# Local attention step with its scale transposes, reciprocals and maxima in another order

## The chip, the cores and the metric

The kernel runs on one core of one Trainium2 chip. The metric is the device time of one execution in microseconds (us). Four compute engines and the DMA queue (SP) each work through a program of their own, in order, and meet only at semaphores: TensorE (PE in the profile, PEld for its weight loads), VectorE (DVE), ScalarE (ACT) and GpSimd (POOL).

## The reference

The input `x` is 4096 x 256. It is layer-normalised to `xn`. A global causal attention with 16 heads of 16 gives `s`. Two layers of local attention with an MLP, each on `xn` or on the result of the layer before, give `g` through a SiLU. The output is `x + s * g`. Everything is float32. The change lies in the local attention, which in the reference is, for each of the two layers:

```python
h = shift_token(x)                    # second half of the features comes from the token before
q, k, v = split(h @ wqkv)             # 8 heads of 64
q = l2norm(q) * qs                    # divided by the root of the sum of squares over the head
k = l2norm(k) * ksc
q, k = rotary_xpos(q, k)
# windows of 128 queries look at their own and the previous 128 keys, masked
attn = softmax(q @ k.T * 8 + mask)
x = x + (attn @ v) @ wo
```

## The kernel before

The program has these parts one after another: projection of the global attention, global attention, local attention layer 1, MLP 1, local attention layer 2, MLP 2, and the gate at the end. Only `local_attention_layer` (called twice) is touched.

It takes the 4096 tokens in 16 steps of 256 (`NI = 16`, two windows of 128 each) and is a software pipeline: each engine has a written-out loop `for k in range(NI + 4)`, and in step `k` it does the projections of tokens `k`, the scale factors and the scores of tokens `k - 1`, and the attention and the output product of tokens `k - 4` and `k - 3`. The order inside the step is written by hand for each engine. Heads are worked on in two halves, `q = 0` and `q = 1`. PSUM is full: `SU` (four banks) holds scores, `BP[0]` and `BP[1]` hold in turn projected queries and keys, their scale factors and the weighted values, and `B6` and `B7` are used in turn for sums, transposes, V and the output product. Each use of a bank waits on the semaphore of the one before.

What each engine does in step `k`, in the order before the change:

- TensorE: `score_max(2k-3)`, the plain scores from which row maxima are taken (L1048); transposes of X into `B7` (L1181); `weigh(k-4, 1)`, the values weighted by the exponentials and their sums for the second half (L1151, sums in `B6`); `score_turned(2k-5)`, the scores once more, keys by queries, with the maxima subtracted (L1065, L1072); `turn_max(2k-3)`, transposes of the maxima into `B7` (L1086); the scale transposes of step `k-1`, four into `BP[0]` and four into `BP[1]` (L1199), each four after a wait for `on` of their half; `values(2k)`, the V product; `project(k, 0)`; `project_out(k-4)`; `project(k, 1)`; `score_max(2k-2)`; `project(k, 2)`, `project(k, 3)`; `values(2k+1)`; `turn_max(2k-2)`; `score_turned(2k-4)`; the sums of squares into `B6` (L1223); `weigh(k-3, 0)` for the first half (sums in `B7`); two transposes of the sums of squares (L1231). The three products of `product3` stand at L79 to L81 for every projection, so those lines are told apart by tile: `a_BP<-a_hTh` is a projection, `a_B<-keep,a_oTh` the output product.
- VectorE: `row_max(2k-3)`, eight maxima (L1260) and, behind them in the same function, the split of the maxima into a high and a low part (L1267, L1269); the low part of `hT`, one column (L1322) and the rest from `B7` (L1325); `divide(k-4, 1)`, the reciprocal of the sums (L1292) and the product `on` (L1296); the scaled queries and keys (L1336); the addition to X (L1304); four `turn`s (rotation, L1286) with `row_max(2k-2)` between the second and third; the copy of the transposed sums of squares out of `B6` (L1352, `ssc`); `divide(k-3, 0)`.
- ScalarE: the high part of `on` for the first half (`high_part(k-4, 0)`, L977), `hT` high (L992, L996), the scale factors spread over 32 columns (L1002, `rnx`), `high_part(k-4, 1)`, `weights(2k-5)`, two exponentials (L949); `turn_max` (L957); `take_v` (L964) and `squares` (L970); `weights(2k-4)`; a copy of the sums of squares (L1025).
- GpSimd: `low_part(k-4, 1)` (L898), masks on the exponentials (`trim`, L907 and L911), the rotation's additions (L926), the power of -0.5 of `ssc` (L932, `rn`), `trim(2k-4, 0)`, `low_part(k-3, 0)`.

The chain of the scale factors runs over four engines: transposes of the sums of squares (TensorE, L1231), copy (VectorE, L1352), power (GpSimd, L932), spreading (ScalarE, L1002), transposes (TensorE, L1199), product (VectorE, L1336). `turn_max` and `values(2k)` on TensorE wait for the low part of `hT` (`hl_done`), `project(k, 0)` for the first product of L1336 (`nrm_done`), `project_out` for the low part of `on` (`olo_done`, L898), `values(2k)` for the reciprocal of the second half (`rec_done`), and `weigh(k-4, 1)` for the copy L1352 of the step before (`ssc_done`).

Of the kernel before, what the change touches and what calls it, by code (L numbers as in the profile page):

```python
# [13 lines left out]
P = 128  # L14
# [773 lines left out]
def local_attention_layer(nc, layer, X, W, WO, w_next, w_o, rope, scale_cols, ident, window_mask, window_rows):  # L788


    with ExitStack() as ctx:
# [15 lines left out]
        id_sb = sb("id", [P, P])  # L807
# [132 lines left out]
        def _(act):  # L940
# [38 lines left out]
            for k in range(NI + 4):  # L979
# [18 lines left out]
                if live(k - 1):  # L998
                    act.wait_ge(rn_done, k)
                    if k >= 2:  # L1000
# [1 line left out]
                    act.activation(rnx[:, :, :, :].rearrange("p a h o -> p (a h) o"),  # L1002
                                   rn[:, :, :, :].rearrange("p a g (h o) -> p (a g h) o", o=1).broadcast_to([P, 2 * 16, HQ]),
                                   ACT.Copy).then_inc(rnx_done, 1)
                high_part(k - 4, 1)
                if win(2 * k - 5):
                    weights(2 * k - 5)
                if win(2 * k - 3):
                    turn_max(2 * k - 3)
                if live(k):  # L1010
# [21 lines left out]
        def _(pe):  # L1032
# [57 lines left out]
            def project(k, g):  # L1090
# [13 lines left out]
                                        hT_hi[:, k % 2, e, tok], hT_lo[:, k % 2, e, tok], e == 0, e == EC - 1)  # L1104
                last.then_inc(p_done, 1)

            def values(n):
                k = n // 2
                if n % 2:
                    pe.wait_ge(vc_done, n)  # L1110
                    if k >= 4:
                        pe.wait_ge(x2_done, k - 3)
                else:
                    pe.wait_ge(hh_done, 2 * (k + 1))
                    pe.wait_ge(hl_done, 2 * (k + 1))
                    if k >= 4:
                        pe.wait_ge(rec_done, 2 * (k - 4) + 2)
                    elif k >= 1:
                        pe.wait_ge(ssc_done, k)
                for e in range(EC):  # L1120
                    lo = 1 - e + (n % 2) * P
                    last = product3(pe, B6[:, :], hT_hi[:, k % 2, e, lo:lo + P], hT_lo[:, k % 2, e, lo:lo + P],
                                    wq_hi[:, e, 2 * INNER:3 * INNER], wq_lo[:, e, 2 * INNER:3 * INNER], e == 0, e == EC - 1)
                last.then_inc(v_done, 1)
# [46 lines left out]
            for k in range(NI + 4):  # L1171
# [13 lines left out]
                    weigh(k - 4, 1)  # L1185
                if win(2 * k - 5):
                    score_turned(2 * k - 5)
                if win(2 * k - 3):
                    turn_max(2 * k - 3)
                if live(k - 1):  # L1190
                    c = k - 1
                    pe.wait_ge(rnx_done, c + 1)
                    for b in range(2):
                        if k >= 4:
                            pe.wait_ge(on_done, 2 * (k - 4) + b + 1)
                        pe.wait_ge(rope_done, 4 * (4 * c + 2 + b + 1))
                        for g in range(2):
                            for a in range(2):
                                last = pe.transpose(BP[b][:, g, a * P:(a + 1) * P],  # L1199
                                                    rnx[:, 4 * a + 2 * b + g, :, :].rearrange("p h o -> p (h o)"), id_sb[:, :])  # L1200
                        last.then_inc(bc_done, 1)
                if live(k):
                    values(2 * k)
                if live(k):
                    project(k, 0)
                    project_out(k - 4)
                    project(k, 1)
# [29 lines left out]
        def _(dve):  # L1237
# [14 lines left out]
            def row_max(w):  # L1252
# [5 lines left out]
                for i in range(4):  # L1258
                    for q in range(2):
                        dve.tensor_tensor_reduce(SU[:, i, q * N2 + lo:(q + 1) * N2], SU[:, i, q * N2 + lo:(q + 1) * N2], mask[:, lo:N2],  # L1260
                                                 1.0, -3.0e38, ALU.add, ALU.max, mx[:, w % 2, i, q:q + 1]).then_inc(max_done, 1)
                dve.wait_ge(max_done, 8 * (w + 1))
                if w >= 2:
                    dve.wait_ge(mt_done, w - 1)
# [21 lines left out]
                    dve.scalar_tensor_tensor(out=dst, in0=src, scalar=s, in1=table, op0=ALU.mult, op1=ALU.mult  # L1286
                                             ).then_inc(rope_done, 1)

            def divide(p, q):
                if live(p):  # L1290
                    dve.wait_ge(av_done, 2 * p + q + 1)
                    dve.reciprocal(rec[:, q, :], (B7, B6)[q][:, 0:N2]).then_inc(rec_done, 1)  # L1292
                    dve.wait_ge(rec_done, 2 * p + q + 1)
                    if p >= 1:
                        dve.wait_ge(olo_done, 2 * (p - 1) + q + 1)
                    dve.tensor_tensor(on[:, 2 * q:2 * q + 2, :], BP[q][:, :, :],  # L1296
                                      rec[:, q, :].rearrange("p (o n) -> p o n", o=1).broadcast_to([P, 2, N2]), ALU.mult
                                      ).then_inc(on_done, 1)
# [7 lines left out]
            for k in range(NI + 4):  # L1306
# [6 lines left out]
                    dve.tensor_tensor(W[1][:, :], scr[:, 0:WCOLS], W[0][:, :].bitcast(F32), ALU.subtract).then_inc(next_low, 1)  # L1313
                if win(2 * k - 3):
                    row_max(2 * k - 3)
                if live(k):
                    dve.wait_ge(hh_done, 2 * k + 2)
                    if k >= 2:
# [24 lines left out]
                    turn(k, 1)  # L1343
                if win(2 * k - 2):
                    row_max(2 * k - 2)
                if live(k):
                    turn(k, 2)
                    turn(k, 3)
                    dve.wait_ge(sst_done, k + 1)
                    if k >= 1:  # L1350
                        dve.wait_ge(rn_done, k)
                    dve.tensor_scalar(ssc[:, :, :, :], B6[:, 0:N2].rearrange("p (a g c) -> p a g c", a=2, g=4)[:, :, :, 0:4],  # L1352
                                      1e-24, None, ALU.max).then_inc(ssc_done, 1)
                divide(k - 3, 0)
                if not live(k):
                    add_out(k - 4)
# [530 lines left out]
```

## Time and profile before

| | us |
|---|---|
| median of 3 runs | 3251.32 (3250.93 to 3257.43) |
| the profiled execution | 3260.36 |
| its span, first to last instruction | 3258.6 |
| mean granted TensorE clock | 0.957 |
| busy: PE | 3008.7 (92%) |
| busy: PEld | 1876.4 (58%) |
| busy: DVE | 2396.2 (74%) |
| busy: ACT | 1714.8 (53%) |
| busy: POOL | 948.3 (29%) |

The profiled execution's time is its span and 1.8 us around it, and it is 9.0 us above the median of the runs. Busy time is the time in which an engine has an instruction at work; weight loads lie beside matmuls. The granted clock is a share of TensorE's full speed. In the timeline the first local layer's steps run from about 1676 us on and the second's to about 2991 us.

### The profile page before, as it was taken

To read this page: it belongs to the slowest core of one execution; us is meant where nothing else is said; L and a number is where in the kernel's file an instruction comes from. 1 tells how busy PE (TensorE), PEld (TensorE's weight loads), DVE (VectorE), ACT (ScalarE), POOL (GpSimd) and SP (SyncE) were. 2 spreads that over 40 slices of the span, in tenths; PEclk is the share of its full clock that TensorE was granted. 3 is DMA by queue.
4 is the path that set the end of the run, shared out by engine and by line. 5 is a ranking of instruction groups with operands and counts; after the bars stand their busy time and mean duration, and the time that the engine had idled before them with its cause. 6 is when DMAs were issued, how large, how long until landed. Compare 5 with 4: busy or idle time off the path is not lost. (4 is left out here: it accounts for less than half of the span.)

```text
span 3258.6 us, 75879 instructions
## 1 busy us (share of the span) xinstructions
PE 3008.7 (92%) x31408; PEld 1876.4 (58%) x31408; DVE 2396.2 (74%) x4034; ACT 1714.8 (53%) x3178; POOL 948.3 (29%) x1006
## 2 busy tenths in 40 slices
PE   7799999999999999999978999987997999986998
PEld 6443333333434333343447787766885787875887
DVE  7689899898779998887526777755655777674666
ACT  4267777788767888888843333322222333332222
POOL 8410000000011000000125555642324555552333
PEclk9699999999989999999979999998998999997999
DMA  7511000100020000000010000001001000001331
GB/s 245 158 38 38 18 10 1 48 18 10 18 62 28 18 10 10 13 13 9 15 34 21 22 19 17 22 21 56 19 7 37 21 15 22 21 28 30 54 90 52
DMA packets 76901, 113.36 MB, mean 35 GB/s; under 512 B 10022, under 2 KB 41636, under 8 KB 76196
## 3 DMA queue, kind: packets, MB, share of 16 engines
q1 hardware_dynamic: 72484, 102.48, 11.1%
q10 hardware_dynamic: 4096, 6.30, 0.7%
q8 instruction: 238, 3.90, 0.5%
q14 instruction: 83, 0.68, 0.1%
HBM read 70.21 MB, written 29.36 MB: 31 GB/s over the span
## 5 line engine op out<-in xcount | busy, mean ns | idle before, releaser
L676 DVE TENSOR_REDUCE mp<-ps_m 128x2 f32<-128x1024 f32 (+3 forms) x1152 | 1275.7, 1134 | 191.5 <-PE ps_m L727 133.1
L649 ACT ACTIVATE probs<-ps_s 128x512 f32<-128x512 f32 (+3 forms) x2304 | 1162.0, 561 | 374.6 <-PE ps_s L751 345.8
L767 PE MATMUL ps_o<-probs,vall 128*32 128x256 f32 (+3 forms) x9216 | 708.0, 379 | 15.3 <-POOL probs L626 9.6
L767 PEld LDWEIGHTS ps_o<-probs,vall 128*32 128x32 f32 x9216 | 185.4, 109 | 340.7 <-issue 177.2
L751 PE MATMUL ps_s<-qst,kst 64*128 64x512 f32 (+3 forms) x1152 | 301.8, 485 | 1.5 <-ACT probs L649 1.2
L751 PE MATMUL ps_s<-qst,keep 64*128 64x512 f32 (+3 forms) x1152 | 293.6, 485 | 3.0 <-ACT probs L649 1.9
L727 PE MATMUL ps_m<-keep,qst 64*128 64x512 f32 (+3 forms) x1152 | 249.4, 420 | 29.5 <-DVE ps_o L664 13.4
L751 PEld LDWEIGHTS ps_s<-qst,kst 64*128 64x128 f32 x1152 | 123.6, 187 | 229.9 <-ACT probs L649 196.0
L610 POOL TENSOR_TENSOR msplit<-negm,mzero 128x16 fp32r<-128x16 f32 x32 | 7.2, 224 | 852.3 <-DVE negm L682 852.3
L626 POOL TENSOR_SCALAR_AFFINE_SELECT probs<-probs 128x256 f32<-128x256 f32 x256 | 102.9, 407 | 508.3 <-ACT probs L649 508.2
L751 PEld LDWEIGHTS ps_s<-qst,keep 64*128 64x128 f32 x1152 | 117.7, 186 | 227.6 <-ACT probs L649 203.0
L926 POOL TENSOR_TENSOR a_rot<-a_scr 128x512 f32<-128x512 f32 x128 | 163.8, 1279 | 284.8 <-DVE a_scr L1286 284.8
L727 PE MATMUL ps_m<-kst,qst 64*128 64x512 f32 (+3 forms) x1152 | 232.3, 382 | 4.1 <-DVE mp L676 3.1
L1260 DVE CUSTOM_DVE_ANT_0 a_SU<-a_SU,a_mask 128x256 f32<-128x256 f32 (+1 forms) x512 | 196.4, 457 | 17.9 <-issue 17.9
L970 ACT ACTIVATE a_scr<-a_BP 128x512 f32<-128x512 f32 x128 | 76.6, 598 | 231.2 <-PE a_BP L81 231.2
L932 POOL TENSOR_TENSOR a_rn<-a_ssc,a_half 128x32 f32<-128x32 f32 x32 | 174.1, 5440 | 76.5 <-DVE a_ssc L1352 76.5
L1286 DVE SCALAR_TENSOR_TENSOR a_scr<-a_BP,a_sc,a_tab 128x256 f32<-128x256 f32 x384 | 166.6, 476 | 27.7 <-ACT a_scr L970 27.4
L977 ACT ACTIVATE a_oTh<-a_on 128x512 fp32r<-128x512 f32 x64 | 40.4, 631 | 264.3 <-DVE a_on L1296 230.5
L1495 ACT ACTIVATE m_gl<-m_bank_u,m_b 128x512 f32<-128x512 f32 x96 | 66.1, 688 | 189.7 <-PE m_bank_u L81 146.5
L1475 POOL TENSOR_TENSOR m_ul<-m_uf,m_uh 128x512 fp32r<-128x512 f32 x80 | 106.1, 1326 | 193.3 <-DVE m_uh L1585 193.3
L949 ACT ACTIVATE a_PT<-a_SU 128x1024 f32<-128x1024 f32 (+1 forms) x128 | 121.8, 1004 | 70.6 <-PE a_SU L1072 70.6
L1292 DVE RECIPROCAL a_rec<-a_B 128x256 f32<-128x256 f32 x64 | 111.8, 1747 | 62.1 <-PE a_B L1151 62.1
(196 smaller groups left out, 5808.1 us busy)
## 6 DMA issues: line engine op xcount, KB each, us to landing
a_tab<-in_rope SPq DMA_DIRECT2D x32, 512.0 KB, 3.6
q_parts<-pparts SPq DMA_DIRECT2D x32, 256.0 KB, 3.9
k_parts<-pparts SPq DMA_DIRECT2D x32, 256.0 KB, 3.9
qst<-q_parts SPq DMA_DIRECT2D x64, 128.0 KB, 2.7
o_raw<-o_sb SPq DMA_DIRECT2D x32, 256.0 KB, 2.1
X<-in_x SPq DMA_DIRECT2D x8, 512.0 KB, 6.7
qst<-q_parts SPq DMA_DIRECT2D x64, 64.0 KB, 2.6
m_xs<-X SPq DMA_DIRECT2D x16, 256.0 KB
```

The source lines that it names most:

```text
L649: act.activation(probs[:, s % PR, h, off:C], sslots[n % SR][:, off:C], ACT.Exp, scale=float(D) ** -0.5).then_inc(exp_done, 1)
L676: dve.tensor_reduce(mp[b % 2][:, h:h + 2, cc:cc + 1], slot[:, :, 0:width], AX.X, ALU.max).then_inc(max_read, 1)
L727: last = pe.matmul(slot[:, x, 0:width], qst[q_slot(b)][rows, hp, a * P:(a + 1) * P], kst[g % 2][rows, hp, cc * C:cc * C + width], start=Tr ...
L751: pe.matmul(sslots[n % SR][:, off:C], kst[g % 2][rows, hp, i * P:(i + 1) * P], qst[q_slot(b)][rows, hp, off:C], start=True, stop=True).the ...
L767: last = pe.matmul(ps_o[32 * h:32 * h + VW, lo:hi], vall[:, i, (g * GH + h) * DV:(g * GH + h) * DV + VW], probs[:, s % PR, h, lo:hi], star ...
L926: pool.tensor_tensor(rot[:, g, :, :].rearrange("p a b -> p (a b)"), t[:, n % 2, 0, :, :].rearrange("p a b -> p (a b)"), t[:, n % 2, 1, :, ...
L932: pool.tensor_tensor(rn[:, :, :, :].rearrange("p a b c -> p (a b c)"), ssc[:, :, :, :].rearrange("p a b c -> p (a b c)"), half[:, :], ALU. ...
L949: act.activation(PT[:, kb % PR, 2 * b:2 * b + 2, :].rearrange("p i (q c) -> p i q c", q=2)[:, :, :, 0:w], SU[:, 2 * b:2 * b + 2, :].rearra ...
L1260: dve.tensor_tensor_reduce(SU[:, i, q * N2 + lo:(q + 1) * N2], SU[:, i, q * N2 + lo:(q + 1) * N2], mask[:, lo:N2], 1.0, -3.0e38, ALU.add, ...
L1286: dve.scalar_tensor_tensor(out=dst, in0=src, scalar=s, in1=table, op0=ALU.mult, op1=ALU.mult).then_inc(rope_done, 1)
L1292: dve.reciprocal(rec[:, q, :], (B7, B6)[q][:, 0:N2]).then_inc(rec_done, 1)
L1475: pool.tensor_tensor(u_lo[:, m, :], uf[:, m % 2, :], u_hi[:, m, :].bitcast(F32), ALU.subtract).then_inc(ul_done, 1)
```

## The change

No instruction is added or removed; the four programs of the local step are put in another order.

- VectorE: `divide` is cut into `invert` (the reciprocal) and `divide` (the product `on`), and `row_max` into `row_max` (the maxima) and `split_max` (the two small instructions). The second half's reciprocal, `invert(k-4, 1)`, goes between the maxima and their split. The first half's, `invert(k-3, 0)`, goes in front of the copy of the sums of squares; both products stay where they were.
- TensorE: the first four scale transposes go in front of `turn_max(2k-3)`, the other four behind `values(2k)`.
- ScalarE: `weights(2k-5)` goes in front of `high_part(k-4, 1)`.

```diff
--- before.py
+++ after.py
@@ -1002,9 +1002,9 @@
                     act.activation(rnx[:, :, :, :].rearrange("p a h o -> p (a h) o"),
                                    rn[:, :, :, :].rearrange("p a g (h o) -> p (a g h) o", o=1).broadcast_to([P, 2 * 16, HQ]),
                                    ACT.Copy).then_inc(rnx_done, 1)
-                high_part(k - 4, 1)
                 if win(2 * k - 5):
                     weights(2 * k - 5)
+                high_part(k - 4, 1)
                 if win(2 * k - 3):
                     turn_max(2 * k - 3)
                 if live(k):
@@ -1103,6 +1103,18 @@
                         last = product3(pe, BP[g % 2][:, d, :], wq_hi[:, e, col:col + P], wq_lo[:, e, col:col + P],
                                         hT_hi[:, k % 2, e, tok], hT_lo[:, k % 2, e, tok], e == 0, e == EC - 1)
                 last.then_inc(p_done, 1)
+
+            def spread_scales(c, b):
+                if live(c):
+                    pe.wait_ge(rnx_done, c + 1)
+                    if c >= 3:
+                        pe.wait_ge(on_done, 2 * (c - 3) + b + 1)
+                    pe.wait_ge(rope_done, 4 * (4 * c + 2 + b + 1))
+                    for g in range(2):
+                        for a in range(2):
+                            last = pe.transpose(BP[b][:, g, a * P:(a + 1) * P],
+                                                rnx[:, 4 * a + 2 * b + g, :, :].rearrange("p h o -> p (h o)"), id_sb[:, :])
+                    last.then_inc(bc_done, 1)
 
             def values(n):
                 k = n // 2
@@ -1185,22 +1197,12 @@
                     weigh(k - 4, 1)
                 if win(2 * k - 5):
                     score_turned(2 * k - 5)
+                spread_scales(k - 1, 0)
                 if win(2 * k - 3):
                     turn_max(2 * k - 3)
-                if live(k - 1):
-                    c = k - 1
-                    pe.wait_ge(rnx_done, c + 1)
-                    for b in range(2):
-                        if k >= 4:
-                            pe.wait_ge(on_done, 2 * (k - 4) + b + 1)
-                        pe.wait_ge(rope_done, 4 * (4 * c + 2 + b + 1))
-                        for g in range(2):
-                            for a in range(2):
-                                last = pe.transpose(BP[b][:, g, a * P:(a + 1) * P],
-                                                    rnx[:, 4 * a + 2 * b + g, :, :].rearrange("p h o -> p (h o)"), id_sb[:, :])
-                        last.then_inc(bc_done, 1)
                 if live(k):
                     values(2 * k)
+                spread_scales(k - 1, 1)
                 if live(k):
                     project(k, 0)
                     project_out(k - 4)
@@ -1259,6 +1261,8 @@
                     for q in range(2):
                         dve.tensor_tensor_reduce(SU[:, i, q * N2 + lo:(q + 1) * N2], SU[:, i, q * N2 + lo:(q + 1) * N2], mask[:, lo:N2],
                                                  1.0, -3.0e38, ALU.add, ALU.max, mx[:, w % 2, i, q:q + 1]).then_inc(max_done, 1)
+
+            def split_max(w):
                 dve.wait_ge(max_done, 8 * (w + 1))
                 if w >= 2:
                     dve.wait_ge(mt_done, w - 1)
@@ -1286,10 +1290,13 @@
                     dve.scalar_tensor_tensor(out=dst, in0=src, scalar=s, in1=table, op0=ALU.mult, op1=ALU.mult
                                              ).then_inc(rope_done, 1)
 
-            def divide(p, q):
+            def invert(p, q):
                 if live(p):
                     dve.wait_ge(av_done, 2 * p + q + 1)
                     dve.reciprocal(rec[:, q, :], (B7, B6)[q][:, 0:N2]).then_inc(rec_done, 1)
+
+            def divide(p, q):
+                if live(p):
                     dve.wait_ge(rec_done, 2 * p + q + 1)
                     if p >= 1:
                         dve.wait_ge(olo_done, 2 * (p - 1) + q + 1)
@@ -1313,6 +1320,9 @@
                     dve.tensor_tensor(W[1][:, :], scr[:, 0:WCOLS], W[0][:, :].bitcast(F32), ALU.subtract).then_inc(next_low, 1)
                 if win(2 * k - 3):
                     row_max(2 * k - 3)
+                invert(k - 4, 1)
+                if win(2 * k - 3):
+                    split_max(2 * k - 3)
                 if live(k):
                     dve.wait_ge(hh_done, 2 * k + 2)
                     if k >= 2:
@@ -1343,14 +1353,18 @@
                     turn(k, 1)
                 if win(2 * k - 2):
                     row_max(2 * k - 2)
+                    split_max(2 * k - 2)
                 if live(k):
                     turn(k, 2)
                     turn(k, 3)
+                    invert(k - 3, 0)
                     dve.wait_ge(sst_done, k + 1)
                     if k >= 1:
                         dve.wait_ge(rn_done, k)
                     dve.tensor_scalar(ssc[:, :, :, :], B6[:, 0:N2].rearrange("p (a g c) -> p a g c", a=2, g=4)[:, :, :, 0:4],
                                       1e-24, None, ALU.max).then_inc(ssc_done, 1)
+                if not live(k):
+                    invert(k - 3, 0)
                 divide(k - 3, 0)
                 if not live(k):
                     add_out(k - 4)
```

## Rows read from the trace of the kernel before

**Rows 1.** Busy time, steady part of layer 1: stretch, length, PE, PEld, DVE, ACT, POOL, clock.

```profile
1720.00:2190.00 470.00, 433.47 (x6446) 359.05 (x6446) 325.75 (x949) 162.23 (x262) 258.69 (x221) 0.97 0.07 20
```

**Rows 2.** TensorE's waits in both layers: who waited for whom, total us, times, longest.

```profile
PEld a_BP L1199 <- DVE a_on L1296: 31.8, 26, 1.3
PEld a_SU L1065 <- DVE a_mx L1260: 27.8, 30, 2.9
```

**Rows 3.** TensorE in one pass, timeline: start us, duration, engine, line, work, [idle before].

```profile
1985.94 1.05 PE L1151 MATMUL a_B<-a_PT,a_ones 128*32 128x128 f32 x24
...
1989.31 0.42 PEld L1181 LDWEIGHTS a_B<-a_id,X 128*128 128x128 f32 x4 [0.41 <-DVE a_rec L1292]
...
1993.12 0.30 PEld L1065 LDWEIGHTS a_SU<-a_negm,a_rowso 32*128 32x128 f32 x8 [0.68 <-DVE a_mx L1260]
...
1995.56 0.20 PEld L1086 LDWEIGHTS a_B<-a_id,a_msp 128*128 128x128 f32 x2
1995.72 0.47 PEld L1199 LDWEIGHTS a_BP<-a_id,a_rnx 128*128 128x128 f32 x4
1997.44 0.42 PEld L1199 LDWEIGHTS a_BP<-a_id,a_rnx 128*128 128x128 f32 x4 [1.25 <-DVE a_on L1296]
...
1999.10 0.19 PEld L79 LDWEIGHTS a_BP<-a_hTh,keep 128*128 128x128 f32 x1
...
2000.75 0.19 PEld L79 LDWEIGHTS a_B<-keep,a_oTh 128*128 128x128 f32 x1
```

**Rows 4.** VectorE in the same pass, timeline.

```profile
1987.40 0.19 DVE L1352 TENSOR_SCALAR a_ssc<-a_B 128x32 f32<-128x32 f32 x1 [4.03 <-PE a_B L1231]
1987.51 1.75 DVE L1292 RECIPROCAL a_rec<-a_B 128x256 f32<-128x256 f32 x1
...
1989.91 0.43 DVE L1260 CUSTOM_DVE_ANT_0 a_SU<-a_SU,a_mask 128x256 f32<-128x256 f32 x1
...
1992.92 0.14 DVE L1260 DVE_READ_ACCUMULATOR2_ANT a_mx<- 128x1 f32 x1
1993.10 0.65 DVE L1267 TENSOR_SCALAR a_msp<-a_mx 128x8 fp32r<-128x8 f32 x1
1993.79 0.55 DVE L1269 SCALAR_TENSOR_TENSOR a_msp<-a_mx,a_msp 128x8 fp32r<-128x8 f32 x1
...
1994.32 0.67 DVE L1325 TENSOR_TENSOR a_hTl<-a_B,a_hTh 128x512 fp32r<-128x512 f32 x1
1994.92 1.74 DVE L1292 RECIPROCAL a_rec<-a_B 128x256 f32<-128x256 f32 x1
1996.69 0.69 DVE L1296 TENSOR_TENSOR a_on<-a_BP,a_rec 128x512 f32<-128x512 f32 x1
1997.30 2.34 DVE L1336 TENSOR_TENSOR a_QK<-a_rot,a_BP 128x1024 f32<-128x1024 f32 x2
...
2018.17 0.19 DVE L1352 TENSOR_SCALAR a_ssc<-a_B 128x32 f32<-128x32 f32 x1 [3.84 <-PE a_B L1231]
```

**Rows 5.** ScalarE in the same pass, timeline.

```profile
1993.15 1.06 ACT L1002 ACTIVATE a_rnx<-a_rn 128x1024 f32<-128x1024 f32 x1 [1.93 <-POOL a_rn L932]
1997.42 0.63 ACT L977 ACTIVATE a_oTh<-a_on 128x512 fp32r<-128x512 f32 x1 [3.21 <-DVE a_on L1296]
1997.95 1.92 ACT L949 ACTIVATE a_PT<-a_SU 128x1024 f32<-128x1024 f32 x2
```

**Rows 6.** GpSimd in the same pass, timeline.

```profile
1987.67 5.45 POOL L932 TENSOR_TENSOR a_rn<-a_ssc,a_half 128x32 f32<-128x32 f32 x1 [2.94 <-DVE a_ssc L1352]
1993.08 0.64 POOL L907 TENSOR_SCALAR_AFFINE_SELECT a_PT<-a_PT 128x512 f32<-128x512 f32 x1
...
1998.13 1.30 POOL L898 TENSOR_TENSOR a_oTl<-a_on,a_oTh 128x512 fp32r<-128x512 f32 x1 [2.58 <-ACT a_oTh L977]
```

**Rows 7.** Timeline of an early pass: GpSimd's power and VectorE's split.

```profile
1743.19 5.44 POOL L932 TENSOR_TENSOR a_rn<-a_ssc,a_half 128x32 f32<-128x32 f32 x1 [1.66 <-DVE a_ssc L1352]
...
1748.10 0.18 DVE L1267 TENSOR_SCALAR a_msp<-a_mx 128x8 fp32r<-128x8 f32 x1
```

## The prediction

> **What bounds the kernel now.** The change touches only the two local attention layers, so I read those. First the busy time by stretch: in the steady part of the first of them TensorE is busy 433 of 470 us at a granted clock of 0.97 of its 2.4 GHz level, VectorE 326, ScalarE 162, GpSimd 259 [rows 1]. TensorE is the bound, and a change of order can win only its idle time. Second, the list of waits, which says where that idle time is. Over both layers TensorE's weight loads wait 31.8 us, 26 times, in front of the second four scale transposes (L1199) for the product `on` of the second half (L1296), and 27.8 us in front of the second score product (L1065) for the row maxima [rows 2]. Third, one pass of the loop in order of time, engine by engine. A pass is 2018.17 - 1987.40 = 30.8 us long [rows 4] and the full passes (k = 4 to 15 in each layer, 24 in all) look alike, so I worked one pass out to the hundredth and multiplied.
>
> In that pass [rows 3] TensorE has four places to look at: X transposes at 1989.31 after 0.41 us of waiting for the first half's reciprocal; score_turned at 1993.12 after 0.68 us of waiting for the maxima; then turn_max at 1995.56 and the first four scale transposes at 1995.72 with no wait; the other four at 1997.44 after 1.25 us of waiting for `on`; the projection at 1999.10. VectorE [rows 4] shows why: the reciprocal of the second half can't start before 1994.92, being queued behind the row maxima, the split of the maxima and the low part of hT, and `on` follows at 1996.69.
>
> **The change, part by part**, on that pass.
>
> *First half's reciprocal ahead of the sums of squares.* It needs the sums that TensorE finishes at 1985.94 + 1.05 = 1986.99 [rows 3], while the copy of the sums of squares (L1352) starts at 1987.40. So the reciprocal runs from about 1987.05 to 1988.80 (before: 1987.51 to 1989.26) and the copy from 1988.80 instead of 1987.40: **1.4 us later**. The product `on` and with it the row maxima start some 0.35 us earlier, 1989.56 in place of 1989.91, and end at 1992.71 in place of 1993.06 [rows 4]. TensorE's wait at L1065 shrinks by that 0.35 and score_turned ends at 1995.21 instead of 1995.56. The 0.41 at the X transposes may shrink too; it lies ahead of the wait at L1065 and pays nothing twice: 0.
>
> The price of it is on the chain of the scales: copy, power of -0.5 on GpSimd (5.45 us from 0.27 after the copy's start), spreading by ScalarE (1.06) [rows 5, 6]. Before, that chain ends at 1993.15 + 1.06 = 1994.21, with 1.5 us to spare. Now it ends at about 1995.65, and the first scale transposes wait for it: 1995.68 - 1995.21 = **0.47 us of new wait**. What is queued behind it on TensorE is everything. The second half's weighting also waits for the copy, now at 1989.0; TensorE gets there at 1989.31 + 0.6, so that wait still costs 0.
>
> *Second half's reciprocal ahead of the split of the maxima.* Its sums are ready when TensorE's weighting ends, before the row maxima do. It runs from 1992.72 to 1994.47 instead of 1994.92 to 1996.66. The split and the low part of hT come behind it, so they are later. Before, these took from 1993.10 to 1994.32 + 0.67 = 1994.99 [rows 4], 1.9 us for some 1.1 us of work, since the two tiny split instructions took 0.65 and 0.55 us there. Where GpSimd runs only its power the first of them takes 0.18 [rows 7]; the long ones match the ends of GpSimd's two mask instructions, 0.64 us each [rows 6]. After the change these masks start when the power ends, near 1994.5, so I expect one or both of the small ones to be held again: hT's low part ends between 1995.7 (none held) and 1996.4 (1.9 us, as before). turn_max and the V product need it.
>
> *TensorE's order.* First transposes 1995.68, four at 0.47 us with their loads, so turn_max could go at 1996.12. With hT's low part at 1996.4 it waits 0.3 us. turn_max takes 0.16 (1995.56 to 1995.72). The V product and the second transposes change places, and their sum stays 1999.10 - 1997.44 = 1.66. So the projection starts between 1996.12 + 0.16 + 1.66 = 1997.94 and 1998.24, against 1999.10. **The gain of a pass is 0.86 to 1.16 us; I take 1.0.** The wait of 1.25 is gone outright: `on` follows the low part by 1997.1, TensorE asks for it at about 1997.6 or later, behind the V product. The projection also asks for the first scaled keys and queries (L1336), 1.2 us behind `on`, at 1998.2 in the late case: just in time, so this is the next thing that is late.
>
> *ScalarE's order.* The exponentials no longer wait for `on`; they start when the spreading ends, 1995.6, take 1.92, and the rounding of `on` starts at 1997.4 to 1997.5, where it stands now (1997.42) [rows 5]. So GpSimd's low part ends at about 1999.43 as before [rows 6]. TensorE comes to the output product, which needs it, at 2000.75 now and at 1999.6 to 1999.9 then: 0 today and 0 then, with 0.2 us of cover left. That is also a ceiling: no pass can win more than about 1.3 us.
>
> Nothing moves past a DMA: the SP queue is untouched, and GpSimd's own order too.
>
> *First and last steps.* For k below 4 there is no reciprocal to move: 0. Step 16 has the wait too, but shorter (26 waits make 31.8 us; 24 of some 1.27 leave 0.65 for each of the other two) [rows 2], and I give it 0.5. The last three steps I leave at 0, between 1 us won and 1 us lost per layer.
>
> *Sum.* 24 x 1.0 + 2 x 0.5 = 25 us. The profiled execution took 3260.36 us and would take 3235; against the median of the runs, 3251.32, which is 9 us below it, the same 25 us give **3226.3 us**, 0.77% less. The wait removed outweighs the one added by a clear margin, and I see no other.
>
> **A rule against the trace.** With the power of -0.5 running from 1743.19 to 1748.63, the split instruction inside it took 0.18 us [rows 7], so in this kernel that GpSimd instruction holds nothing of VectorE. The Trainium skill (SBUF — State Buffer, section SBUF: two separate sides) says that the port pair shared by VectorE and GpSimd is an exclusive lock, held for the whole instruction by whichever starts first. By that rule the split behind the moved reciprocal would stand until the power ends, some 0.05 us here, and the sum would be 1 us less; the trace disagrees for the power and agrees for the masks.
>
> **The rivals.**
>
> *A: half the gain.* Two covers are thin: 0.2 us at the output product, and in the late case hardly any at L1336. If instructions need 0.1 to 0.2 us more at each hand-over than I counted, five hand-overs of the scale chain and the low part eat half of 1.0: 0.5 x 24 = 12 us, 3239. For it: I counted hand-overs of 0.03 to 0.08 us from few rows. Against: the same pairs stand in the trace with these gaps.
>
> *B: no change.* The scale chain, 1.4 us later, takes back everything: this needs its end at about 1996.7, 1.0 us later than worked out, 3251. Against it: both durations on it are steady. The change not doing what it says belongs here.
>
> *C: slower.* GpSimd's instructions queue back to back from 1994.5 on: two masks and a low part of 1.28 us [rows 6]. If each of VectorE's three small instructions (two splits, the one-column copy of hT) loses its turn to the next GpSimd instruction, the low part of hT starts behind all three, at 1997.1, and ends at 1997.75. turn_max then goes at 1997.8 and the projection at 1999.6, 0.5 us later than now: 24 x 0.5 = 12 us lost, 3263. It decides from the point at which hT's low part ends after 1997.25. For it: the two splits are held in just this way now. Against it: the copy of hT now starts at the edge of that 1.28 us instruction and VectorE goes on at once, with the next instruction at 1994.32.
>
> **How the numbers follow.** Forecast (0.8 to 1.25 us per pass, 3220 to 3232) 0.62; A 0.16; still more (the X transposes' wait and the last steps pay as well, 3216) 0.08; B 0.06; C 0.08. Faster by over 0.2%, which is 6.5 us and about what a measurement of this kernel can tell from no change: 0.62 + 0.16 + 0.08 = 0.86. Same 0.06, slower 0.08. The range holds the forecast, A and the larger gain: 3216 to 3243, the upper end being A with 4 us for the spread of the runs (3250.93 to 3257.43).
>
> **What would show it.** In the changed profile: no wait of L1199 for L1296; L1065's wait for the maxima down from 0.68 to about 0.33 us; a new wait of L1199 for the spreading L1002, about 0.5 us, 24 times; turn_max (L1086 in the old numbering) waiting 0 to 0.3 us for hT's low part; the pass 29.8 us long instead of 30.8; the power of -0.5 starting 1.4 us later against the weighting. I am wrong if the new wait is over 1 us, if hT's low part comes after 1997.25 in the terms of this pass, or if a wait appears at the output product.

## The result and the profile after

The changed kernel takes 3214.45 us (median of 4 runs, 3210.76 to 3217.11) against 3251.12 us (4 runs, 3250.01 to 3257.43): 36.7 us less by the medians, and by the ratio of 0.988 (95% interval 0.987 to 0.989) some 39. I had forecast 3226.3, 25 us less, in a range of 3216 to 3243. The direction was right and the size too small.

The profiled execution took 3213.5 us. The kernel is still bound by TensorE, and in the list of waits these two lines are the answer to [rows 2] (weight loads, whole kernel: total us, times, longest; L1115 is the old L1199, L1002 the spreading, L1262 the row maxima):

```profile
PEld a_BP L1115 <- ACT a_rnx L1002: 42.5, 30, 6.7
...
PEld a_SU L1065 <- DVE a_mx L1262: 18.4, 30, 2.9
```

The wait for `on` of [rows 2], 31.8 us, is gone; the wait for the maxima fell from 27.8 to 18.4; the one for the spread scale factors rose from 15.2 to 42.5. The timeline of one full pass, TensorE first (to be held against [rows 3]; L1233 are the transposes of the sums of squares, which in the pass before start at 1986.92):

```profile
1999.01 0.20 PEld L1233 LDWEIGHTS a_B<-a_id,a_sse 128*128 128x128 f32 x2 [0.20 <-issue]
...
2004.77 0.30 PEld L1065 LDWEIGHTS a_SU<-a_negm,a_rowso 32*128 32x128 f32 x8 [0.32 <-DVE a_mx L1262]
...
2007.61 0.42 PEld L1115 LDWEIGHTS a_BP<-a_id,a_rnx 128*128 128x128 f32 x4 [0.79 <-ACT a_rnx L1002]
2008.00 0.25 PEld L1086 LDWEIGHTS a_B<-a_id,a_msp 128*128 128x128 f32 x2
...
2010.04 0.19 PEld L79 LDWEIGHTS a_BP<-a_hTh,keep 128*128 128x128 f32 x1
...
2011.48 0.19 PEld L79 LDWEIGHTS a_B<-keep,a_oTh 128*128 128x128 f32 x1
```

The timeline of VectorE in the same pass (L1296 reciprocals, L1364 the copy of the sums of squares, L1271 and L1273 the split, L1335 hT's low part), against [rows 4]:

```profile
1999.15 1.76 DVE L1296 RECIPROCAL a_rec<-a_B 128x256 f32<-128x256 f32 x1 [3.49 <-PE a_B L1163]
2000.83 0.13 DVE L1364 TENSOR_SCALAR a_ssc<-a_B 128x32 f32<-128x32 f32 x1
...
2004.79 1.76 DVE L1296 RECIPROCAL a_rec<-a_B 128x256 f32<-128x256 f32 x1
2006.46 0.11 DVE L1271 TENSOR_SCALAR a_msp<-a_mx 128x8 fp32r<-128x8 f32 x1
2006.61 0.49 DVE L1273 SCALAR_TENSOR_TENSOR a_msp<-a_mx,a_msp 128x8 fp32r<-128x8 f32 x1
...
2007.09 0.67 DVE L1335 TENSOR_TENSOR a_hTl<-a_B,a_hTh 128x512 fp32r<-128x512 f32 x1
```

And of GpSimd, against [rows 6]:

```profile
2001.03 5.44 POOL L932 TENSOR_TENSOR a_rn<-a_ssc,a_half 128x32 f32<-128x32 f32 x1 [4.00 <-DVE a_ssc L1364]
2006.43 0.64 POOL L907 TENSOR_SCALAR_AFFINE_SELECT a_PT<-a_PT 128x512 f32<-128x512 f32 x1
...
2009.98 1.29 POOL L898 TENSOR_TENSOR a_oTl<-a_on,a_oTh 128x512 fp32r<-128x512 f32 x1 [1.06 <-ACT a_oTh L977]
```

From the transposes of the sums of squares to the output product it is 2011.48 - 1999.01 = 12.47 us; before, 2000.75 - 1986.92 = 13.83. That is 1.36 us of a pass. The length of a pass can be read free of everything else as the spacing of GpSimd's powers, first and last of 11 passes in a row. The timeline of GpSimd in the kernel before, first power and last:

```profile
1802.45 5.44 POOL L932 TENSOR_TENSOR a_rn<-a_ssc,a_half 128x32 f32<-128x32 f32 x1 [2.93 <-DVE a_ssc L1352]
...
2141.87 5.44 POOL L932 TENSOR_TENSOR a_rn<-a_ssc,a_half 128x32 f32<-128x32 f32 x1 [2.73 <-DVE a_ssc L1352]
```

And in the changed kernel:

```profile
1794.44 5.44 POOL L932 TENSOR_TENSOR a_rn<-a_ssc,a_half 128x32 f32<-128x32 f32 x1 [4.20 <-DVE a_ssc L1364]
...
2119.12 5.44 POOL L932 TENSOR_TENSOR a_rn<-a_ssc,a_half 128x32 f32<-128x32 f32 x1 [4.01 <-DVE a_ssc L1364]
```

A pass took (2141.87 - 1802.45) / 11 = 30.86 us and takes (2119.12 - 1794.44) / 11 = 29.52: **1.34 us less**, in both layers, where I had taken 1.0. In each layer 12 passes of this kind make 16 us. From the first power to the start of the last addition to X, a layer went from 531.5 to 512.2 us (the second: 531.6 to 511.6; its last addition starts at 2997.1 us of the timeline before).

For the steps at the two ends the power is a bad mark. From step 3 on it stands 2.02 us behind the transposes of the sums of squares in the changed kernel, and 0.75 us behind them before. Counted between those transposes on TensorE, the first three steps went from 77.3 to 77.1 us in the first layer and from 77.4 to 78.2 in the second: 0.3 won and 0.8 lost. What follows the transposes of step 15 went from 84.6 to 81.5 and from 84.6 to 79.9: 3.0 and 4.8 us won.

The times of one kernel spread by 10 us and more, and the profiles show where: the global attention, which no edit touches, had its last exponential at 1666.9 us before and at 1658.0 after. So below, the length of a pass decides, and the timed ratio stands beside it. The length comes from one profiled execution of each kernel, as a mean over 11 passes; the second layer gives the same within 0.02 us in each.

### The profile page after: what moved, and what is told of

The parts are those of the page before. It is cut to its first block and busy times, and to the rows that moved or that the text cites. A ratio compares the mean times of both kernels' runs of the same rounds, so it can differ in the third digit from the quotient of the medians.

```text
span 3211.8 us, 75885 instructions
## 1 busy us (share of the span) xinstructions
PE 2985.6 (93%) x31408; PEld 1866.3 (58%) x31408; DVE 2377.4 (74%) x4034; ACT 1712.5 (53%) x3178; POOL 950.7 (30%) x1006
## 5 line engine op out<-in xcount | busy, mean ns | idle before, releaser
L1296 DVE RECIPROCAL a_rec<-a_B 128x256 f32<-128x256 f32 x64 | 112.5, 1757 | 154.4 <-PE a_B L1163 152.9
L1262 DVE CUSTOM_DVE_ANT_0 a_SU<-a_SU,a_mask 128x256 f32<-128x256 f32 (+1 forms) x512 | 196.4, 457 | 12.3 <-issue 12.3
L727 PEld LDWEIGHTS ps_m<-keep,qst 64*128 64x128 f32 x1152 | 118.4, 195 | 64.9 <-DVE mp L676 46.8
```

The lines of the kernel that those rows point to most:

```text
L727: last = pe.matmul(slot[:, x, 0:width], qst[q_slot(b)][rows, hp, a * P:(a + 1) * P], kst[g % 2][rows, hp, cc * C:cc * C + width], start=Tr ...
```

## The experiments

The reasons of the prediction can be taken apart, since the change has four parts: the first half's reciprocal (A), the second half's reciprocal (B), TensorE's order (C) and ScalarE's (D). First each was taken back alone, then some were tried alone. The kernel before ran beside each group.

| kernel | parts | full pass, us | ratio to before (95%) |
|---|---|---|---|
| before | none | 30.86 | 1 |
| changed | A B C D | 29.52 | 0.988 (0.987 to 0.989) |
| e1 | B C D | 30.13 | 0.996 (0.994 to 0.997) |
| e2 | A C D | 29.52 | 0.989 (0.987 to 0.991) |
| e3 | A B D | 29.76 | 0.991 (0.988 to 0.994) |
| e4 | A B C | 29.76 | 0.989 (0.988 to 0.991) |
| e5 | C D | 30.14 | 0.995 (0.993 to 0.997) |
| e6 | A | 29.62 | 0.991 (0.989 to 0.993) |
| e7 | B | 30.55 | 0.997 (0.995 to 0.999) |
| e8 | A with sums first, C D | 29.13 | 0.985 (0.983 to 0.987) |
| e9 | B C D in the last steps only | 30.87 | 0.999 (0.997 to 1.000) |
| e10 | e8, by step | 29.14 | 0.986 (0.984 to 0.988) |
| e11 | none, GpSimd's order | 30.06 | 0.995 (0.992 to 0.997) |

**e1, A taken back.**

```diff
                     turn(k, 3)
-                    invert(k - 3, 0)
                     dve.wait_ge(sst_done, k + 1)
...
-                if not live(k):
-                    invert(k - 3, 0)
+                invert(k - 3, 0)
                 divide(k - 3, 0)
```

> The changed kernel, but the first half's reciprocal goes behind the copy of the sums of squares again. Theory (the two ends meet): the new wait for the spread scale factors (0.53 to 0.79 us a pass) goes, the wait for the row maxima goes from 0.32 back to 0.67 us, and the first scale transposes start where they started; a pass stays at 29.5 +- 0.2 us and the time at 3210 to 3220 us. Rival (this part pays, since it lets VectorE's small instructions slip past GpSimd's): hT's low part is late by some 0.5 us again, a pass 30.0 us, 3226. Other rival (this part costs, as its new wait says): a pass 28.9 us, 3199.

Measured: 30.13 us a pass, 0.61 more than the changed kernel, and 3237.0 us beside 3252.8 for the kernel before. My theory fell. The first rival stands in the pass (30.0 us expected); its 3226 us were too few. What A does can be seen in the timeline of VectorE in e1, next to that of the changed kernel above:

```profile
1981.71 0.99 DVE L1271 TENSOR_SCALAR a_msp<-a_mx 128x8 fp32r<-128x8 f32 x1
1982.73 0.18 DVE L1273 SCALAR_TENSOR_TENSOR a_msp<-a_mx,a_msp 128x8 fp32r<-128x8 f32 x1
...
1982.91 0.68 DVE L1335 TENSOR_TENSOR a_hTl<-a_B,a_hTh 128x512 fp32r<-128x512 f32 x1
```

GpSimd in e1:

```profile
1974.80 5.45 POOL L932 TENSOR_TENSOR a_rn<-a_ssc,a_half 128x32 f32<-128x32 f32 x1 [2.92 <-DVE a_ssc L1363]
1980.20 0.64 POOL L907 TENSOR_SCALAR_AFFINE_SELECT a_PT<-a_PT 128x512 f32<-128x512 f32 x1
1980.80 0.64 POOL L911 TENSOR_SCALAR_AFFINE_SELECT a_PT<-a_PT 128x512 f32<-128x512 f32 x1
1981.40 1.27 POOL L898 TENSOR_TENSOR a_oTl<-a_on,a_oTh 128x512 fp32r<-128x512 f32 x1
```

TensorE in e1, first scale transposes and turn_max:

```profile
1982.68 0.42 PEld L1115 LDWEIGHTS a_BP<-a_id,a_rnx 128*128 128x128 f32 x4
1983.71 0.20 PEld L1086 LDWEIGHTS a_B<-a_id,a_msp 128*128 128x128 f32 x2 [0.61 <-issue]
```

Without A the power ends at 1980.2, so the masks and the low part that follow it on GpSimd are done by 1982.67. The first split instruction, issued at 1981.71 beside the low part, stands until exactly then (0.99 us instead of 0.18), hT's low part ends at 1983.59, and turn_max goes at 1983.71 after 0.61 us of idling. The row names no releaser for it; but it goes 0.12 us behind the end of hT's low part in every full pass of e1, and in the changed kernel 0.24 us or more behind. With A the power ends at 2006.4, and the first split instruction is through beside its end in 0.11 us; only the second is held, to 0.49, until the first mask ends at 2007.07. (The row of that mask starts 0.03 us ahead of the first split instruction, which is not held all the same; what happens in that overlap is open.)

**e2, e3, e4: B, C and D taken back, one each.** The edits restore the lines of the diff: `invert(k - 4, 1)` directly in front of `divide(k - 4, 1)` (e2), turn_max in front of all eight scale transposes (e3), `high_part(k - 4, 1)` in front of `weights(2k-5)` (e4).

> The changed kernel, but the second half's reciprocal goes behind the split of the maxima and hT's low part again. Theory: with the first half's reciprocal early, the split falls wholly beside the power and takes 0.18 + 0.18 us, hT's low part is ready 1.8 us earlier, the reciprocal ends at about 8.7 us after the transposes of the sums of squares, and the V product asks for it at 9.2: nothing lost, a pass 29.5 us, 3214 +- 4. Rival (this part is what removed the wait for `on`): the wait comes back for the most part, 0.8 us or more a pass, 3234 or more.

> The changed kernel, but TensorE has its old order: turn_max, all eight scale transposes, then the V product. Theory: `on` is ready about 9.35 us after the transposes of the sums of squares, and the second four transposes come up at 9.3: 0.2 us a pass lost, 3219 +- 4. Rival (TensorE's order is the main part, since it covers the wait with the V product): 1.2 us a pass lost, 3243.

> The changed kernel, but ScalarE rounds `on` before the exponentials again. Theory: `on` is there earlier than before, both have cover, no pass changes; the last steps give back up to 1 us per layer: 3214 to 3217. Rival (the output product's cover is thin and this order decides it): a wait at the output product either way of more than 0.2 us a pass, a change of 5 us or more.

Measured: 29.52, 29.76 and 29.76 us a pass. B is worth nothing once A and C are there; C is worth 0.24, as expected for e3. D is worth 0.24 as well, where I expected nothing: in the pass, its rival stands. What D moves is the copy of V on ScalarE (L964). The output product writes the same bank and waits for that copy (`vc_done`), a wait that I had left out. Before the change:

```profile
2000.02 0.61 ACT L964 ACTIVATE a_V<-a_B 128x512 f32<-128x512 f32 x1
```

In e4, ScalarE and then TensorE:

```profile
2009.74 0.61 ACT L964 ACTIVATE a_V<-a_B 128x512 f32<-128x512 f32 x1
```

```profile
2010.46 0.19 PEld L79 LDWEIGHTS a_B<-keep,a_oTh 128*128 128x128 f32 x1 [0.17 <-issue]
```

In e4 the copy ends at 2010.35 and the product starts 0.11 us later; before, it ends at 2000.63 and the product starts at 2000.75. In 22 full passes each of the kernel before, e6, e9 and e11 the product starts 0.11 to 0.12 us behind the end of the copy, and in the changed kernel 0.78 to 0.82. So the copy, queued behind the exponentials, which wait there for the rounding of `on`, holds the product; this is read from the timing, since no run moves the copy alone. The timed ratios of e4 and the changed kernel can't be told apart.

**e5, e6, e7: C with D, A, and B alone.**

> The kernel before with TensorE's and ScalarE's new order alone, both reciprocals where they were. Theory (the moves overlap; each alone brings most of a pass's gain or little): the V product now waits for the second half's reciprocal, at 1996.7 in the pass shown of before, and the output product starts 0.75 us earlier than before: a pass 30.1 us, 3233 +- 5. Rival (the reciprocals are the change and TensorE's order only spends the time they free): no gain, 3251.

> The kernel before with the first half's reciprocal in front of the copy of the sums of squares alone. Theory: the power now covers the split of the maxima, which takes 0.18 + 0.18 instead of 0.65 + 0.55 us; with the maxima 0.35 earlier, `on` is ready at 1996.3 instead of 1997.3 and the second four transposes follow at 1996.35: a pass 29.8 us, 3224 +- 5. Rival (the delay of the power is a cost that only the other parts outweigh): the scale chain eats it, a pass 30.5 or more, 3243 or more.

> The kernel before with the second half's reciprocal ahead of the split of the maxima alone. Theory: the split now begins beside GpSimd's low part (1.27 us) and stands until that ends, hT's low part is ready near 1996.5 instead of 1995.0, turn_max waits about 1 us for it, and little is left of the gain of 1.25 us: a pass 30.5 us, 3243 +- 5. Rival (this part removes the wait for `on`, as I had it in the prediction): 1 us a pass, 3226.

Measured: 30.14, 29.62 and 30.55 us a pass; the theory stands in all three as far as the pass goes, A's gain being larger than expected (29.8). (The kernel before took 3256 us in this group, so the ratios count, not the times.) **A alone brings 1.24 of the 1.34 us.** The timeline of VectorE in e6, where only the one reciprocal is moved:

```profile
1999.43 0.18 DVE L1271 TENSOR_SCALAR a_msp<-a_mx 128x8 fp32r<-128x8 f32 x1
1999.65 0.17 DVE L1273 SCALAR_TENSOR_TENSOR a_msp<-a_mx,a_msp 128x8 fp32r<-128x8 f32 x1
...
1999.83 0.68 DVE L1334 TENSOR_TENSOR a_hTl<-a_B,a_hTh 128x512 fp32r<-128x512 f32 x1
```

GpSimd in e6:

```profile
1995.71 5.44 POOL L932 TENSOR_TENSOR a_rn<-a_ssc,a_half 128x32 f32<-128x32 f32 x1 [4.01 <-DVE a_ssc L1364]
```

The split falls wholly beside the power, which ends at 2001.15, and takes 0.18 and 0.17 us. From its start to that of hT's low part it is 1999.83 - 1999.43 = 0.40 us, where the kernel before has 1994.32 - 1993.10 = 1.22: 0.82 us of A's 1.24. Of the rest, the maxima give about what I had counted: TensorE waits 0.32 us for them instead of 0.68. In e7 it is the opposite. Its timeline has the split on VectorE:

```profile
1981.11 0.98 DVE L1271 TENSOR_SCALAR a_msp<-a_mx 128x8 fp32r<-128x8 f32 x1
```

and on GpSimd the low part beside it:

```profile
1980.79 1.27 POOL L898 TENSOR_TENSOR a_oTl<-a_on,a_oTh 128x512 fp32r<-128x512 f32 x1
```

The split stands until the low part ends, and in e7's list of waits the wait that left `on` is back in front of turn_max, 49.4 us where the kernel before had 16.5:

```profile
PEld a_B L1086 <- DVE a_msp L1273: 49.4, 32, 4.1
```

**e11, the cause by itself.** If GpSimd's masks and low part hold the split, moving them alone must help, with VectorE, TensorE and ScalarE as before (both low parts wait for the rounding of the second half):

```diff
             for k in range(NI + 4):
+                low_part(k - 4, 0)
                 low_part(k - 4, 1)
+                trim(2 * k - 6, 0)
                 trim(2 * k - 6, 1)
...
-                trim(2 * k - 4, 0)
-                low_part(k - 3, 0)
```

> The kernel before in all but one thing: GpSimd's masks and low part that stand right behind the power go behind the rounding of the second half, so that nothing of GpSimd runs beside the split of the maxima. No instruction of VectorE, TensorE or ScalarE is moved. Theory (those instructions hold the split): the split takes 0.18 + 0.18 us, `on` is ready 0.85 us earlier, the wait for it falls from 1.25 to 0.4 us, a pass 30.0 us, 3231 +- 5. Rival (the split's length comes from something else, the maxima it reads for one): 0.65 + 0.55 us as before, a pass 30.85, 3251, or more where the low parts are late for the output product.

The timeline of e11, VectorE:

```profile
1990.02 0.18 DVE L1267 TENSOR_SCALAR a_msp<-a_mx 128x8 fp32r<-128x8 f32 x1
1990.23 0.17 DVE L1269 SCALAR_TENSOR_TENSOR a_msp<-a_mx,a_msp 128x8 fp32r<-128x8 f32 x1
...
1992.79 0.69 DVE L1296 TENSOR_TENSOR a_on<-a_BP,a_rec 128x512 f32<-128x512 f32 x1
```

GpSimd, nothing between the power and the low parts:

```profile
1984.59 5.45 POOL L934 TENSOR_TENSOR a_rn<-a_ssc,a_half 128x32 f32<-128x32 f32 x1 [2.92 <-DVE a_ssc L1352]
1994.22 2.55 POOL L898 TENSOR_TENSOR a_oTl<-a_on,a_oTh 128x512 fp32r<-128x512 f32 x2 [4.19 <-ACT a_oTh L977]
```

TensorE, the second four scale transposes:

```profile
1993.53 0.42 PEld L1199 LDWEIGHTS a_BP<-a_id,a_rnx 128*128 128x128 f32 x4 [0.42 <-DVE a_on L1296]
```

Every number came as the theory said: 0.18 and 0.17 us for the split, 0.42 us of wait for `on` instead of 1.25, a pass of 30.06. That the split was held by these GpSimd instructions is shown, and that freeing it is worth 30.86 - 30.06 = 0.80 us a pass with VectorE's order as it was, some two thirds of what A brings.

**e9, the last steps alone** (old order for `k < NI`, new for `k >= NI`):

> The kernel before in steps 0 to 15 and the changed order from step 16 on. Theory (the last steps are worth something of their own, which the prediction put at about 1 us): step 16 gains from the second reciprocal, from TensorE's order and from TensorE's clock not falling as far, 2 to 4.5 us a layer; passes stay at 30.85 us; 3251 less 4 to 9. Rival (that gain comes from the full passes before it): step 16 stays at 45.2 us, 3251.

Passes 30.87, and a layer of 528.3 and 528.4 us instead of 531.5 and 531.6: 3.2 us each, within what was expected; the timed ratio leaves open whether there is any gain. From the transposes of step 15 on, e9 won 3.5 and 3.4 us where the changed kernel won 3.0 and 4.8, so the gain of the last steps needs nothing of the full passes. Part of it goes with TensorE's clock. The timeline of TensorE has step 16's plain and turned scores (L1048, L1072), in the kernel before:

```profile
2153.46 3.48 PEld L1048 LDWEIGHTS a_SU<-a_QK 32*128 32x128 f32 x64 [2.08 <-issue]
...
2162.31 3.11 PEld L1072 LDWEIGHTS a_SU<-a_QK 32*128 32x128 f32 x32
```

in the changed kernel:

```profile
2127.73 2.05 PEld L1048 LDWEIGHTS a_SU<-a_QK 32*128 32x128 f32 x64 [0.96 <-issue]
...
2134.86 2.90 PEld L1072 LDWEIGHTS a_SU<-a_QK 32*128 32x128 f32 x32
```

and the busy time by stretch around them, before:

```profile
2150.00:2160.00 10.00, 4.92 (x74) 4.23 (x72) 5.87 (x20) 2.73 (x4) 4.80 (x7) 0.83 0.00 0
2160.00:2170.00 10.00, 9.11 (x127) 6.58 (x128) 1.25 (x6) 2.33 (x3) 1.22 (x2) 0.66 0.01 2
```

and after:

```profile
2126.00:2136.00 10.00, 5.54 (x104) 4.75 (x106) 5.86 (x21) 2.65 (x5) 5.80 (x8) 0.90 0.01 2
2136.00:2146.00 10.00, 10.00 (x164) 8.14 (x160) 3.22 (x5) 2.57 (x3) 2.49 (x3) 0.93 0.01 2
```

The granted clock (the third value from the end) is 0.83 and 0.66 before and 0.90 and 0.93 after: in a step without projections TensorE had stood idle for 2.08 us in front of the scores, and loaded them in 3.48 us; now it stands for 0.96 and takes 2.05. In e9 these rows are (L1051 being its L1048):

```profile
2143.86 2.01 PEld L1051 LDWEIGHTS a_SU<-a_QK 32*128 32x128 f32 x64 [0.80 <-issue]
```

That is 3.48 - 2.01 = 1.47 us of e9's 3.5 in the first layer. The turned scores take 3.11 us in e9 as before, so there the clock won nothing back. Idle time alone doesn't decide it: e7 stood idle for 2.03 us at this place in both layers and loaded the scores in 3.41 us in the first and 1.91 in the second. How the rest of the gain divides was not separated.

**e8 and e10, beyond the change.** A delays the copy of the sums of squares. That cost goes if the first half's reciprocal can start earlier still:

```diff
-                for d in range(3):
+                for d in ((2, 0, 1) if q == 0 else (0, 1, 2)):
...
+                    if q == 0 and d == 2:
+                        last.then_inc(sum_done, 1)
```

and `invert(p, 0)` waits for `sum_done`, `divide` for `av_done`; B is taken back.

> The changed kernel with the second half's reciprocal back behind hT's low part, and in the weighting of the first half the sums come before the values, with a semaphore of their own, on which the first half's reciprocal waits. The reciprocal then ends before the sums of squares are transposed, and delays their copy by nothing. Theory: the wait for the spread scale factors (0.53 to 0.79 us) falls to the 0.33 us that a change from tiled to full products leaves, everything else holds: a pass 29.1 us, 3203 +- 5. Rival (the power, 1.4 us earlier, brings GpSimd's masks and low part under the split and hT's low part is held): a pass 29.5 to 30, 3214 or more.

The timeline of TensorE in e8, transposes of the sums of squares and first scale transposes:

```profile
2002.73 0.20 PEld L1235 LDWEIGHTS a_B<-a_id,a_sse 128*128 128x128 f32 x2 [0.20 <-issue]
...
2010.77 0.42 PEld L1115 LDWEIGHTS a_BP<-a_id,a_rnx 128*128 128x128 f32 x4 [0.33 <-issue]
```

VectorE in e8, reciprocal and copy:

```profile
2001.13 1.76 DVE L1301 RECIPROCAL a_rec<-a_B 128x256 f32<-128x256 f32 x1 [1.76 <-PE a_B L1163]
2003.20 0.19 DVE L1370 TENSOR_SCALAR a_ssc<-a_B 128x32 f32<-128x32 f32 x1 [0.32 <-PE a_B L1235]
```

The reciprocal starts 1.6 us ahead of the transposes, the copy is late by nothing, and the first scale transposes come after 0.33 us of waiting: 29.13 us a pass, as expected. What is late now is the output product: it starts at 2014.80, 0.06 us behind the end of GpSimd's low part (2013.45 + 1.29 = 2014.74). e8's last steps gave some back (from the addition to X of step 16 to that of step 17: 22.9 instead of 21.3 us), which e10 was to mend:

> The kernel with the sums first, in each step with the order that is best there: TensorE's old order in steps 1 to 3 (where turn_max otherwise stands behind the long wait for the scale factors), sums first and the second reciprocal late in steps 4 to 15, the changed kernel's order from step 16 on. Theory: passes 29.13 as there, step 16 at 40.7 and step 17 at 21.3, the first steps 1 to 1.5 us shorter: 5 to 6 us less per layer than the changed kernel, ratio to before 0.984 to 0.985. Rival (the first and last steps depend on where TensorE's clock falls and give nothing reliable): ratio 0.986 to 0.988.

e10 has 29.14 a pass and 3206.7 us (3205.0 to 3208.1), the lowest median of all, but its layers are 505.7 and 510.5 us long, so against e8 (510.6 and 510.8) the gain of the steps at the ends came in one layer only. Its ratio of 0.986 is what the rival said, and its interval overlaps with the changed kernel's. Both e8 and e10 have shorter passes than either kernel; that the whole is faster than the changed kernel is likely and, by the timed ratios, not settled.

## Why the prediction fell short

- *The bound.* Right: TensorE's idle time was what could be won, and in the full passes every gain that was traced is a wait that went.
- *The pass, 1.0 us.* **This term was too small:** it measured 1.34 (1.36 in the pass shown). The difference adds up from four terms. The first scale transposes came 0.16 us earlier than I worked out (8.60 us after those of the sums of squares, against 8.76): right behind the reciprocal the copy takes 0.13 us instead of 0.19, and the power follows it closer. hT's low part came at the early end of my bounds (8.75, against 8.8 to 9.5), so turn_max waited for nothing, where I had put in 0.16 as a mean. The V product and the second transposes did not keep their sum of 1.66: with the transposes behind the V product's 512 columns it is 2010.04 - 2008.21 = 1.83, 0.17 lost. And I measured the gain at the first projection, 1.15 us earlier. From there to the output product it was 1.65 us and is 1.44: the first projection no longer stands behind the V product, and the output product no longer waits for V's copy, where I had counted no wait. 1.0 + 0.16 + 0.16 - 0.17 + 0.21 = 1.36. The gain should have been read at the next wait, not at the next instruction.
- *The ceiling of 1.3 us.* Not one: GpSimd's low part did not end as before but 0.25 us earlier (12.26 us after the transposes of the sums of squares, against 12.51), and the output product starts 0.21 us behind it, the cover that I had given it. e8 won 1.73 a pass, and there that cover is used up.
- *Which part pays.* **This step failed as I put it.** I costed A as an even trade, 0.35 us won at the maxima for 0.47 us of new wait, and gave the gain to B and C. The runs say the reverse: A alone brings 1.24 us (e6), B alone 0.3 (e7), and B, C and D without A 0.73 (e1). I had seen that the split was held by the masks, but asked only whether it would still be held behind B; that A moves the power over the old place of the split, and so frees it (0.8 us, e6 and e11), was in the same rows. Each part found its wait removed by another: that is why taking B away costs nothing.
- *The new wait of L1115.* Right in place, and so was the end of the wait for `on`. It shows as some 0.79 us in 18 of the 26 passes from step 3 on and as 0.53 in the other 8, where I forecast 0.47; but these loads show 0.33 us in front of them in e8 too, where they wait for nothing.
- *The port rule.* The split beside the power took 0.11 to 0.18 us, and beside masks or low part up to 0.99. The Trainium skill (SBUF — State Buffer, section SBUF: two separate sides) says that a GpSimd instruction that starts first has the port pair shared with VectorE for its whole length. The runs agree for the masks (0.65 and 0.55 us before, 0.18 and 0.17 in e11) and the low part (0.99 in e1), and not for the power (0.18 and 0.17 inside its 5.44 us in e6).
- *The last steps, 0.5 us a layer.* **This term failed as well.** They gave 3.0 and 4.8 us, and 3.5 and 3.4 in e9, which changes nothing ahead of them. I had given step 16 only its share of the wait for `on` and left the other three at 0, although TensorE has no projections there to cover a wait; and some 1.4 us of it are loads that ran at a higher granted clock.
- *The sum.* Two layers: 24 x 0.34 = 8 us more from passes, 7 more from the last steps and 0.5 less from the first three, against 25: 39 to 40, which is what the two layers lost (19.3 + 20.0); the medians say 36.7. Rival A (half the gain), B (no change) and C (slower) did not come; the case of a larger gain, which I gave 0.08, did, by the last steps as I had said there but not by the X transposes, and went past its end.

## What to carry to other kernels

When an instruction takes several times its usual time, find what ran beside it and ask of each moved instruction whether it brings the two together or apart; a shift of 1.3 us on one engine was worth 0.8 us a pass here by the company it changed, about twice the 0.4 us that was still to be had by taking its delay away (29.52 against 29.13 in e8). Parts of a reorder often remove the same wait, so price them one at a time and together. And look at the first and last steps of a software pipeline by themselves: they have less to cover a wait with.

## What the runs showed of the hardware

- VectorE's two split instructions (128x8, all operands in SBUF) took 0.17 to 0.18 us beside GpSimd's power of 5.44 us (e6, e11), and 0.49 to 0.99 us beside its masks (0.64) or its subtraction (1.27), ending 0.03 us after these (before, changed, e1).
- VectorE's 128x32 copy took 0.19 us when its engine had been idle (before, e8) and 0.13 right behind a reciprocal (changed).
- In the kernel before, an idle stretch of 2.08 us before 64 weight loads went with a granted clock of 0.66 to 0.83 in the 20 us around and after them, and the loads took 3.48 us; after 0.96 us of idling they took 2.05. In e7 they took 3.41 us in one layer and 1.91 in the other after the same 2.03 us.
